# A convolution and attention kernel on one core: group means and the values projection moved in the order of work, exponentials of the last steps kept in wide SBUF buffers

## What is computed

```
x = x + L0(gn(x))
    t  = silu(bn(conv1x1(x)))                      # 512 channels
    ys = [t[:, :256], t[:, 256:]]
    for i in 0, 1:                                 # two bottlenecks
        z = silu(bn(conv3x3(ys[-1])))              # 256 channels
        q, k, v = conv1x1(z), 4 heads of 64, 1024 positions
        a = softmax(q . (k + rw + rh) / 8);  z = a . v
        z = silu(bn(conv1x1(z)));  ys.append(ys[-1] + z)
    out = silu(bn(conv1x1(concat(ys))))            # 1024 to 512 channels
x = x + L1(gn(x))                                  # masked 1x1 convolution, channels permuted
```

## Time and profile before

| | us |
|---|---|
| median of 3 runs | 3354.56 (3351.9 to 3355.57) |
| the profiled execution | 3349.9 |
| its span on the core | 3347.9 |
| PE busy | 3072.6 (92%) |
| DVE busy | 1871.9 (56%) |
| ACT busy | 1568.1 (47%) |
| POOL busy | 1047.1 (31%) |

### The profile page before, as it was taken

How to read it: one execution, slowest core, us unless ns; L and a number is a source line. 1 busy time by engine, 2 the same in 40 slices (tenths; PEclk the granted TensorE clock), 3 DMA queues, 4 the chain that set the end, 5 groups by cost and what they waited for, 6 DMA issues and landing times.

```text
span 3347.9 us, 61223 instructions
## 1 busy us (share of the span) xinstructions
PE 3072.6 (92%) x27308; PEld 1574.6 (47%) x27308; DVE 1871.9 (56%) x2515; ACT 1568.1 (47%) x1826; POOL 1047.1 (31%) x768
## 2 busy tenths in 40 slices
PE   3769999999998999999999999989999899999997
PEld 3524554454544545445444545435454454445453
DVE  5536465375654656455653657546564657537464
ACT  1315465173732746245651737327362455517382
POOL 1113451052511443134411525105431244115051
PEclk8889999999999999999999999999999999999998
DMA  4200000100011000100001000110001000000001
GB/s 144 73 26 30 1 30 26 64 17 29 11 51 44 2 29 23 54 29 2 30 26 51 30 29 8 38 60 2 29 20 57 29 1 30 26 26 30 1 8 44
DMA packets 35894, 105.60 MB, mean 32 GB/s; under 512 B 12976, under 2 KB 15024, under 8 KB 32944
## 3 DMA queue, kind: packets, MB, share of 16 engines
q1 hardware_dynamic: 35632, 101.69, 8.5%
HBM read 80.18 MB, written 21.50 MB: 30 GB/s over the span
## 4 chain that ended last, share of the span: by engine, by line
PE 76%; DVE 11%; ACT 6%; issue 4%; POOL 3%; SPq 0%; DMA 0%; POOLq 0%; DVEq 0%
PE ps_u L679 48%; PE ps_u L838 12%; DVE row_max L1199 4%; PE ps_o L860 4%; PE ps_o L861 3%; PE ps_o L862 3%; ACT wide L986 3%; PE ps_u L812 3%; PE ps_u L698 2%; DVE stats L1133 1%; POOL y_pad L1307 1%; ACT ps_u L986 1%; DVE qk L1188 1%; POOL z L1307 1%; PE ps_u L870 1%
## 5 line engine op out<-in xcount | busy, mean ns | idle before, releaser
L679 PE MATMUL ps_u<-y_pad,w_c 128*128 128x512 f16 x3456 | 792.7, 387 | 0.0
L1199 DVE TENSOR_REDUCE row_max<-ps_u 128x2 f32<-128x1024 f32 x512 | 617.5, 1220 | 189.7 <-PE ps_u L812 189.7
L1333 POOL TENSOR_TENSOR probs<-wide,probs 128x1024 f16<-128x1024 f32 x256 | 544.9, 2128 | 515.5 <-ACT probs L990 504.8
L1007 DVE SCALAR_TENSOR_TENSOR wide<-wide 128x512 f32<-128x512 f32 x256 | 182.5, 715 | 655.1 <-ACT wide L906 653.3
L679 PEld LDWEIGHTS ps_u<-y_pad,w_c 128*128 128x128 f16 x3456 | 333.0, 98 | 424.9 <-issue 28.0
L905 ACT ACTIVATE wide<-ps_u,par_m_t 128x512 f32<-128x512 f32 x128 | 99.3, 776 | 863.7 <-PE ps_u L679 863.7
L838 PE MATMUL ps_u<-qk 64*128 64x512 f16 x3072 | 418.7, 378 | 41.4 <-ACT shift_rows L978 19.6
L860 PEld LDWEIGHTS ps_o<-v_ext,probs 128*128 128x128 f16 x4096 | 375.9, 96 | 143.4 <-issue 128.9
L860 PE MATMUL ps_o<-v_ext,probs 128*128 128x65 f16 x4096 | 431.4, 193 | 0.0
L861 PE MATMUL ps_o<-v_ext,probs 128*128 128x64 f16 x4096 | 429.1, 195 | 0.0
L862 PE MATMUL ps_o<-v_ext,probs 128*128 128x65 f16 x4096 | 426.5, 192 | 0.0
(11 more groups left out here) (182 smaller groups left out, 3933.4 us busy)
## 6 DMA issues: line engine op xcount, KB each, us to landing
w_c<-w_c_dram SPq DMA_DIRECT2D x15, 2304.0 KB, 8.9
xn<-in_x_dram SPq DMA_DIRECT2D x32, 512.0 KB, 5.7
o_nat<-in_x_dram SPq DMA_DIRECT2D x64, 256.0 KB, 2.6
out_dram<-qk SPq DMA_DIRECT2D x32, 512.0 KB, 2.7
w_c_dram<-w_c SPq DMA_DIRECT2D x2, 2304.0 KB, 8.0
qk<-in_L_conv_m_cv_w_dram SPq DMA_DIRECT2D x2, 1152.0 KB, 7.1
probs<-in_L_conv_m_cv_w_dram SPq DMA_DIRECT2D x2, 1152.0 KB, 10.8
probs<-in_L_conv_cv_w_dram SPq DMA_DIRECT2D x2, 1024.0 KB, 12.0
```

Of the source, the lines that this page charges most:

```text
L679: ins = e.matmul(o, lhsT, rhs, start=start and k == 0, stop=stop and k == len(pairs) - 1)
L1199: e.reduce_max(row_max[:, g % 2, :, it, half], ps_u[:, use.slot:use.slot + 2, :], axis=AX.X).then_inc(*dve_max.up(i, b, g, half, it))
L1333: e.tensor_tensor(p_part(s, 1), wide[:, w.slot, :], p_part(s, 0), ALU.subtract).then_inc(*pool_lo.up("p", i, b, s))
```

## The change

Three edits. The group-mean product of the next image is planned behind conv_end(0,1) and no longer behind conv_end(1,0), and the variance product behind conv_end(1,1). The projection v(3) moves from before the eighth maximum to behind the shift row; q(0,1) takes its place, with two maxima behind it. The steps from 24 on take a wide buffer for their exponential: ACT writes it there, rounds it from there, and DVE subtracts from there; their PSUM banks are free after the exponential, and the planner holds them for 1.4 instead of 4.2.

```diff
-        NORM_PARTS = {(0, 0, 0): 1, (0, 0, 1): 1, (0, 1, 0): 1, (0, 1, 1): 0, (1, 0, 0): 2, (1, 0, 1): 1, (1, 1, 0): 1, (1, 1, 1): 0}
+        NORM_PARTS = {(0, 0, 0): 1, (0, 0, 1): 0, (0, 1, 0): 1, (0, 1, 1): 1, (1, 0, 0): 2, (1, 0, 1): 1, (1, 1, 0): 1, (1, 1, 1): 0}
         HALF_0 = (("q", 1, 0), ("k", 1, 0), ("v", 0), ("v", 1))
-        HALF_1 = ((("k", 0, 1), 0), (("v", 2), 1), (("k", 1, 1), 2), (("v", 3), 1), (("q", 0, 1), 0))
+        HALF_1 = ((("k", 0, 1), 0), (("v", 2), 1), (("k", 1, 1), 2), (("q", 0, 1), 2))
...
                 for _ in range(count):
                     next(maxima)
-                if at == ("v", 3):
-                    next(maxima)
             plan_shift_row(i, b, 0)
+            piece("v", 3)
             next(maxima)
...
                 if way(s)[1] == "pool":
                     w = wide_ring.take(("pool_lo", ("p", i, b, s)))
+                elif s >= LAST_MAX + 2:
+                    w = wide_ring.take(("dve_lo", ("p", i, b, s)))
                 freed_by, hold = (("act_exp", (i, b, s)), 1.4) if w else (("dve_lo", ("p", i, b, s)), 4.2)
...
-                late = None if w else (i, b, s, use)
+                late = (i, b, s, use, w) if way(s)[1] == "vector" else None
...
-                    i, b, s, use = a
+                    i, b, s, use, w = a
                     e.wait_ge(*act_cast.at("p", i, b, s))
-                    e.tensor_tensor(p_part(s, 1), both(use), p_part(s, 0), ALU.subtract).then_inc(*dve_lo.up("p", i, b, s))
+                    e.tensor_tensor(p_part(s, 1), wide[:, w.slot, :] if w else both(use), p_part(s, 0), ALU.subtract).then_inc(*dve_lo.up("p", i, b, s))
...
-                    if w is None:
+                    if way(s)[1] != "pool":
                         continue
```

## The result

The changed kernel took 3359.94 us, median (3357.8 to 3365.0), where the kernel before took 3353.78 beside it: a ratio of 1.0019, interval [1.0012, 1.0027]. That is 6.2 us more, just inside the 0.2% that I called no change, and outside my range of 3316 to 3356. The sign of the forecast was wrong.

A forecast was written before the change was run, and what follows sets the result against it. The prediction took TensorE's order of work, 76% of the chain, as the bound. Its terms, -47.6 + 24.0 + 9.6 = -14.0 us, gave 3340.6 us, with a range of 3316 to 3356.

The forecast's parts named there:

- The sign of the forecast: Whole kernel: the change makes it faster, by 14.0 us; chance of faster 0.72.
- Part 1, the means: Group-mean product: PE's wait and the half clock behind it go, 6.8 us an image, 47.6 us in seven.
- Rival (d): Group means: only the idle time of the wait goes, net -1.0 us, 3354 us; chance 0.06.
- Part 2, the values projection: Start of attention: DVE's order makes it wait for v3, 1.5 us in each of 16 bottlenecks, 24.0 us lost.
- Rival (a): Start of attention: v3 is free or fills PE's gaps, net -38 us, 3316.6 us; chance 0.12.
- rival (b): Start of attention: PE's clock falls to half at each, 1.7 us in 16, net +13 us, 3368 us; chance 0.08.
- Part 3, the wide buffers: Last steps: step 28 waits for the residual tile's buffer, plus POOL contention; 0.6 us in each of 16, 9.6 us lost.
- My upper end: Last steps: both subtractions stretched by some 0.4 us, 1.2 us a bottleneck, 19 us lost.
- The sum: Whole kernel: means -47.6, values projection +24.0, wide buffers +9.6, together -14.0 us, so 3340.6 us.
- rival (c): Last steps and values projection both cost their upper ends, 19 and 29 us: net 0.4 us, 3355 us; chance 0.12.

The follow-up runs named there:

- e1_means: The kernel before with the moved group-mean and variance products alone: 3304.23 us against 3351.54, ratio 0.9857.
- e12_v3_fill: e2_v3 with six unused matmuls of 512 columns added in PE's idle time ahead of each first shift row: 3380.59 us, ratio 1.0087 to the kernel before.
- e11_psum_29: The changed kernel with the values projection put back and step 29's exponential alone left in PSUM: 3324.07 us, ratio 0.9913 to the kernel before.
- e8_psum_27_29: The changed kernel with the values projection put back and the exponentials of steps 27 and 29 left in PSUM: 3306.43 us, ratio 0.9853 to the kernel before.
- e7_lo_first: The changed kernel with the values projection put back and the residual tile's last reader planned ahead of step 27's subtraction: 3309.99 us, ratio 0.9864.
- e2_v3: The kernel before with the values projection's move alone: 3397.68 us, ratio 1.0137.
- e5_fill: The changed kernel with six unused matmuls of 512 columns added in PE's idle time ahead of each first shift row: 3352.01 us, ratio 0.9992 to the kernel before.
- e3_wide: The kernel before with the wide buffers from step 24 alone: 3377.77 us, ratio 1.0078.

## Why the prediction was wrong, step by step

**Part 1, the means: right.** 6.8 us an image were forecast, 47.6 in seven; the trace has 6.86 in the images with a bottleneck before them and 45.6 in all, and e1_means alone measured 47.3. PE's waits at line 748 (749 in after) fell from 9 to 2. The half clock behind them went with them, and the variance product in its new place showed no cost, as I took it. Rival (d) is out.

**Part 2, the values projection: the order right, the clock missing.** I forecast 1.5 us in each of 16 by DVE's order, 24.0; the runs show 1.52, 24.3 (e12_v3_fill by itself, and after where the clock stays up). Rival (a) is out. What failed is the step by which I put rival (b) aside: "the stretch from 1066 to 1086 has 4.7 us of idle time and stays at 1.00". That sum says how much PE idles, not how the idle time lies. In before it is in pieces, with q(0,1)'s matmuls between the last maximum and the shift. The timeline of PE in before, third image:

```profile
1072.01 0.39 PE L812 MATMUL ps_u<-qk 64*128 64x512 f16 x2 [0.83 <-DVE row_max L1199]
1072.33 1.47 PE L679 MATMUL ps_u<-z,w_qkv 128*128 128x512 f16 x6
1073.85 0.41 PE L821 MATMUL ps_u<-ident_shift,shift 128*64 128x128 bf16 x8
```

The move takes the six matmuls out and leaves one piece of 1.51 us, with two logits matmuls and another wait of 0.83 us ahead of it. I had named that hole in rival (b), then gave it 0.08 and put the clock at nothing in the sum. It happened in 10 bottlenecks of 16, at 1.07 us each where I priced 1.7: 10.7 us, under the 14.0 from which I had it decide the sign; with the last steps beside it, it did.

The Trainium skill ("TensorE: Matmul & The Clock Gate", A second HAM failure mode: psum-queue depth-cycling) tells of a kernel in which short idle times between groups of matmuls make the clock go up and down. This case's trace agrees: half clock behind waits of 0.83 and 1.51 us in 10 of 16 places, and none there in e12_v3_fill, with the second one filled.

**Part 3, the wide buffers: the mechanism right, the size halved.** ACT waits for line 1240 in every bottleneck (17 waits in the view), and PE for the subtraction of step 29, as forecast. I had 0.6 us in each, 9.6; it is 1.25, 20.0. The mis-sized term is the contention with POOL, which I took as 0.14, a third of 0.42, once. The row shows 0.36 on step 27 (1.58 where 1.22), and that one lies ahead of line 1240, so it lengthens ACT's wait and all behind it; and 0.29 on step 29. By these rows 0.5 of the missing 0.65 us is this; no run takes the stretch of step 27 away with the wait left in place, and e11_psum_29, which takes away that of step 29, wins 0.1 us a bottleneck, since another wait shows. e8_psum_27_29 shows that the residual's buffer and these two subtractions together are all there is, and e7_lo_first that 0.90 of it hangs on when the buffer comes free. My upper end, 1.2 for two stretched subtractions, was the value.

The Trainium skill ("SBUF — State Buffer", Who interferes with whom) calls the port pair that DVE and GpSimd share an exclusive lock, and says that issue order decides who blocks. In the rows DVE, which comes second, isn't held for all of the overlap: of the 0.53 us that its subtraction at 1140.25 overlaps with POOL's pass (until 1140.78) it lost 0.36, and of the 0.44 at 1146.87 it lost 0.29.

**The sum.** -45.6 + 24.3 + 10.7 + 20.0 + 1.5 (the end and the steps between) = 10.9 in the trace of after, where I had -47.6 + 24.0 + 9.6 = -14.0. Of the 24.9 between them 10.7 is the clock, 10.4 the last steps. Neither alone would have turned the sign; rival (c) had the second and no case had both, though nothing excludes one by the other. The range ended at 3356 because I left rival (b) out of it and let its clock and the last steps' upper end occur one at a time. By the medians, +6.2, the miss is 20.2 us, less by the 4.8 us by which the two profiled executions stand off their medians.

**What stays open.** Why the clock falls in 10 bottlenecks of after and in 15 of e2_v3, with the same waits at the shift row in both, and why its moment there ranges from 0.7 us ahead of the shift row to 1.3 us behind it: the waits alone don't set it. What brings the late falls: two in after, three in e2_v3, four in e5_fill with the filler, none in e12_v3_fill. And why the half clock behind the means' wait lasts longer in e2_v3, e3_wide and e12_v3_fill (up to 131.70 us for the stretch in the first and 131.30 in the second, where 130.36).

## What to carry to other kernels

A projection that fills a wait does two things: it is work that must be done somewhere, and, as here, it can keep TensorE at its clock where it stands. Before moving it, write down the idle pieces that it leaves and their lengths, not only their sum, and follow the order of the engine that sets the pace to see when it asks for the moved result. A ring of buffers lent to a new user makes that user wait for the slowest old one; look for that holder, and for which of its readers stand behind instructions that the edit itself makes longer. Measure the parts of a change apart: here one part was worth 47.3 us (3304.23, the best kernel of all) and the two others took more than that.

## What the runs showed of the hardware

- The granted clock fell to half behind 1.51 us of idle time with PE busy on short work around it: in 10 of 16 places in one kernel, in 15 of 16 in another with the same waits; some falls came 5.5 to 5.8 us behind it. Six matmuls of 512 columns (1.47 us) in the idle piece kept it at 1.00 in all 16 of e12_v3_fill and brought 17 us; in e5_fill they took away the eight falls at the idle piece, and four late ones came where after had two.
- A subtraction of DVE of 1024 elements takes 1.22 us with one operand in PSUM and 1.22 with both in SBUF; with two SBUF operands beside a pass of POOL of 0.62 us it took 1.51 to 1.58. From PSUM beside the same pass it stayed at 1.22 (e11_psum_29, step 29).
